# The end of the multi-head graph stage: TensorE's loop runs to the last chunk, its last heads stand between the last stage's first products, and sums and statistics move forward

## The reference

```python
x = _L0_gnn_ref(x, adj, ...)   # layer norm, 8-head attention, + Wo; layer norm, gelu(h Wf1) Wf2; residuals
# _L1_gnn_ref(x, bias=adj, ...)
attn_in = layer_norm(x, g1, b1)
attn = graph_attention(attn_in, bias, W1, a_src1, a_dst1) + x      # 8 heads of 32
attn_in2 = layer_norm(attn, g2, b2)
out = graph_attention(attn_in2, bias, W2, a_src2, a_dst2) + attn   # 1 head of 256
# graph_attention: h = x W; s = h.a_src; t = h.a_dst
#   softmax(leaky_relu(s_i + t_j, 0.2) + bias) @ h
```

## Time and profile before

| | |
|---|---|
| median of three runs | 1089.6 us |
| the profiled execution | 1089.35 us, of which the span of instructions 1087.5 us |
| PE busy | 1042.4 us, 96% of the span |
| DVE, ACT, POOL busy | 799.3, 713.7, 406.7 us |
| mean granted clock of PE | 0.990 |

### The profile page before, as it was taken

The page is one execution under the profiler, slowest core; times in us unless marked ns, Lnnn a source line. Parts: engine busy times, 40 slices in busy tenths (PEclk is TensorE's granted clock), DMA queues, the critical chain, the costliest instruction groups (busy, mean ns, idle before and its releaser), DMA issues.

```text
span 1087.5 us, 39257 instructions
## 1 busy us (share of the span) xinstructions
PE 1042.4 (96%) x15958; PEld 917.0 (84%) x15958; DVE 799.3 (74%) x1919; ACT 713.7 (66%) x1724; POOL 406.7 (37%) x642
## 2 busy tenths in 40 slices
PE   8999999999999998999999999999889999869997
PEld 7888888888888877899889988998778888768886
DVE  5677777777777787866665666545779988859996
ACT  4876777777677764544554455546678888847774
POOL 3711211211111113411131113212368888767773
PEclk9999999999999999999999999999999999989999
DMA  8211112211110002100110011010001000001222
GB/s 234 69 41 42 41 42 65 56 41 42 41 41 18 6 10 59 33 21 21 30 29 20 21 30 30 20 40 11 14 20 30 19 19 29 4 2 60 79 78 98
DMA packets 78520, 43.67 MB, mean 40 GB/s; under 512 B 38926, under 2 KB 74028, under 8 KB 78380
## 3 DMA queue, kind: packets, MB, share of 16 engines
q1 hardware_dynamic: 78360, 41.72, 14.1%
q10 hardware_dynamic: 20, 0.01, 0.0%
HBM read 21.25 MB, written 12.58 MB: 31 GB/s over the span
## 4 chain that ended last, share of the span: by engine, by line
PE 83%; issue 4%; DVE 4%; POOL 3%; SPq 3%; ACT 2%; DMA 1%; POOLq 0%; DVEq 0%; ACTq 0%
PE BK L1436 8%; PE BK L1438 8%; PE BK L1437 8%; PE BK L1588 6%; PE BK L1562 5%; PE BK L1717 5%; PE BK L1718 5%; PE BK L1719 5%; PE BK L1574 4%; PE BK L1555 3%; PE BK L1461 3%; PE BK L1452 3%; PE BK L1764 3%; PE BK L1886 2%; PE BK L1453 2%
## 5 line engine op out<-in xcount | busy, mean ns | idle before, releaser
L1270 ACT ACTIVATE gf<-BK,bcol 128x512 f32<-128x512 f32 x128 | 88.4, 691 | 156.4 <-PE BK L1438 143.2
L1041 POOL TENSOR_TENSOR ve<-mv,eps_l 128x4 f32<-128x4 f32 x64 | 18.1, 283 | 454.1 <-DVE mv L323 435.6
L1190 ACT ACTIVATE e_sb<-BK,nmx 128x128 f32<-128x128 f32 x512 | 142.4, 407 | 28.5 <-DVE nmx L535 28.5
L632 DVE TENSOR_TENSOR gl<-gf,gh 128x512 fp32r<-128x512 f32 x128 | 100.9, 790 | 64.3 <-ACT gh L1271 62.0
L1717 PE MATMUL BK<-wf_hi,gh 128*128 128x256 f32 x512 | 142.3, 278 | 0.3 <-DVE gl L632 0.2
L1718 PE MATMUL BK<-wf_hi,gl 128*128 128x256 f32 x512 | 141.7, 277 | 0.0
L1719 PE MATMUL BK<-wf_lo,gh 128*128 128x256 f32 x512 | 141.6, 277 | 0.0
L541 DVE TENSOR_TENSOR pt_sb<-BK,ft 128x512 f32<-128x512 f32 x128 | 85.2, 686 | 56.0 <-PE BK L1562 54.4
L1210 ACT ACTIVATE xn<-x_all,neg_mr,rstd 128x256 f32<-128x256 f32 (+1 forms) x188 | 103.4, 608 | 5.1 <-POOL neg_mr L1050 4.7
L1436 PE MATMUL BK<-xh,wf_hi 128*128 128x512 f32 x256 | 101.5, 396 | 2.8 <-DVE xl L352 2.8
L1438 PE MATMUL BK<-xh,wf_lo 128*128 128x512 f32 x256 | 101.5, 397 | 0.0
(11 more groups left out here) (214 smaller groups left out, 2768.0 us busy)
## 6 DMA issues: line engine op xcount, KB each, us to landing
out_dram<-y SPq DMA_DIRECT2D x16, 512.0 KB, 2.9
x_all<-in_x_dram SPq DMA_DIRECT2D x15, 512.0 KB, 4.6
xn<-tb_ln SPq DMA_DIRECT2D x240, 32.0 KB, 1.9
adj_in<-in_adj_dram SPq DMA_DIRECT2D x64, 64.0 KB, 3.5
adj_kept<-adj_tr SPq DMA_DIRECT2D x16, 256.0 KB, 2.5
adj_in<-adj_kept SPq DMA_DIRECT2D x16, 256.0 KB, 2.6
s_wf<-in_L_gnn_Wf_dram SPq DMA_DIRECT2D x2, 1024.0 KB, 7.4
x_all<-in_x_dram SPq DMA_DIRECT2D x2, 256.0 KB, 2.9
```

The source lines that it names most:

```text
L632: dve.tensor_tensor(gl[:, f, :], gf[f % 2][:], gh[:, f, :].bitcast(F32), ALU.subtract).then_inc(b_gl, 1)
L1190: e = act.activation(e_sb[:, j, :], LE[:, r, q, :], ACT.Exp, bias=nmx[:, j:j + 1], scale=1.0)
```

## The change

On PE the loop of the multi-head stage covers all chunks but the first two (`tail=0`); behind it the remaining heads of chunk 14 go around the ratios, the turn of chunk 1 for the last stage comes earlier, and the last four heads of chunk 15 stand in pairs between the high and the low products of the last stage's chunk 0. The wait for all of chunk 15's output copies (`c_ev`) moves from ahead of the last stage to its step 1.

On POOL the bias and the scale for chunk 2 (addition to chunk 0, L1018, and L1041 to L1050) move from behind both residuals to between those of chunk 14 and chunk 15. On DVE the aggregation and the next statistics move forward too, and a wait for POOL's last share of chunk 15 (`c_att`) comes in before step 1 writes y. DVE caps the row of chunk 1 instead of POOL. On ACT the normalisation of chunk 1 comes before the copies of chunk 14.

In the feed-forward stage, step 0 makes the low part of chunk 1, and normalises and turns chunk 2, after one addition instead of two; the marks come after the fourth addition, and the sums and scores in steps 1 and 2. The high parts of W1 and W2 (ACT) and their low parts (POOL) come one step later.

```diff
@@ DVE, feed-forward
-                    if g == 2 and not final:
+                    if g == (1 if i == 0 else 2) and not final:
                         turned_lo(i + CB + 1)
...
-                    if isinstance(i, int) and i == 0 and g < 2:
-                        (setup_marks, lambda: setup_sums(0, 0))[g]()
+                    if isinstance(i, int) and i == 0 and g == 3:
+                        setup_marks()
                     if isinstance(i, int) and i == 1 and g < 3:
-                        (lambda: setup_sums(0, 1), lambda: setup_scores(0), lambda: setup_sums(1, 0))[g]()
-                    if isinstance(i, int) and i == 2 and g < 2:
-                        (lambda: setup_sums(1, 1), lambda: setup_scores(1))[g]()
+                        (lambda: setup_sums(0, 0), lambda: setup_sums(0, 1), lambda: setup_scores(0))[g]()
+                    if isinstance(i, int) and i == 2 and g < 3:
+                        (lambda: setup_sums(1, 0), lambda: setup_sums(1, 1), lambda: setup_scores(1))[g]()
@@ DVE, end of the multi-head stage
             for h in range(4):
                 c_scale(NC - 1, h)
+            dve.wait_ge(ln_nm, nm_count(CD + 1, CD))
+            dve.wait_ge(ln_st, (CD + 3) * G)
+            aggr(CD + 2)
             c_recip(NC - 2, 1 - last)
...
             d_lo(1, 1, 1)
+            dve.wait_ge(ln_mv, (CD + 3) * G)
+            for g in range(G):
+                stats(CD + 3, 3, g)
             c_recip(NC - 1, last)
@@ DVE, last stage (the same work is taken out of step 0)
                 d_bias(i, par)
+                if at == 1:
+                    dve.wait_ge(c_att, NC * G + C_START)
...
-                if i == 0:
+                if i < 2:
                     d_cap(i)
@@ POOL
+                    if first == CD and i == 0:
+                        return
...
                     residual_sum(NC - 2)
+                    add_bias(0, CD, c2_bc, d_xb)
+                    pool.wait_ge(ln_xn, (CD + 2) * G)
+                    rstd_of(CD + 2, EPS[CD])
+                    neg_mean_of(CD + 2, CD)
                     residual_share(NC - 1, (NC - 1) % 2)
@@ ACT
+            normalise(0, CD, range(G))
             c_out_copy(NC - 2, 1 - last, 1)
             c_out_copy(NC - 2, 1 - last, 2)
-            normalise(0, CD, range(G))
-            c_out_copy(NC - 1, last, 0)
             d_hi(1, 1, 0)
             d_hi(1, 1, 1)
+            c_out_copy(NC - 1, last, 0)
@@ PE
-            looped(pe, c1_step)
+            looped(pe, c1_step, tail=0)
...
+            def first_product(g):
+
+                pe.wait_ge(c_pp, (NC - 1) * H + g + 6)
+                d_h_hi(0, 0, g)
+                d_h_hi(0, 0, g + 1)
```

More of the change, by code:

```diff
@@ L850, in c2_step @@
                 prev = (i - 1, half - (1 - par), 1 - par)
-                if ahead:
+                if ahead and i > 0:
                     dve.wait_ge(ln_nm, nm_count(i + CD + 1, CD))
@@ L855, in c2_step @@
                     d_norms(*older, 2, 3)
-                if ahead:
+                if ahead and i > 0:
                     aggr(i + CD + 2)
-                if far:
+                if far and i > 0:
                     dve.wait_ge(ln_mv, (i + CD + 3) * G)
@@ L1014, in add_bias @@
                 for g in range(G):
-                    if first == CD and g == 2 and i > 1:
+                    if first == CD and g == 2 and i > 2:
                         pool_cap(i - 1)
@@ L1094, in norms @@
                         setup_gain("w2", 28)
-                    if first == CB and isinstance(i, int) and i == 1:
+                    if first == CB and isinstance(i, int) and i == 2:
                         setup_lo("w1", False, 3)
@@ L1293, in b_step @@
                     turned_hi(i + CB + 1)
-                if isinstance(i, int) and i == 0:
+                if isinstance(i, int) and i == 1:
                     setup_hi("w1", False, 5)
@@ L1821, in _ @@
             pe.wait_ge(setup_pool, 7)
-            looped(pe, c1_step)
+            looped(pe, c1_step, tail=0)
             last = (NC - 1) % 2
+            c_av(NC - 2, 1 - last, 4)
+            c_av(NC - 2, 1 - last, 5)
             pe.wait_ge(ln_xl, (CD + 1) * KT)
             ratios(NC - 1, last, 0)
-            for h in range(4, H):
-                c_av(NC - 2, 1 - last, h)
-            ratios(NC - 1, last, 1)
-            for h in range(4):
-                c_av(NC - 1, last, h)
+            c_av(NC - 2, 1 - last, 6)
+            c_av(NC - 2, 1 - last, 7)
             pe.wait_ge(c_hb, NC * 2)
@@ L1833, in _ @@
             d_ln_turn(1, 1, 1)
-            for h in range(4, H):
-                c_av(NC - 1, last, h)
+            ratios(NC - 1, last, 1)
             def d_h_hi(i, par, g):
@@ L1890, in c2_step @@
                 more = back and not (isinstance(i, int) and i == NC - 1)
-                d_h_pair(i, par, 0)
+                if i == 1:
+                    pe.wait_ge(c_ev, NC * len(HEAD_GROUPS))
                 if back:
+                    d_h_pair(i, par, 0)
                     d_outer(i - 1, 1 - par)
-                d_h_pair(i, par, 2)
+                    d_h_pair(i, par, 2)
                 if back:
@@ L1903, in c2_step @@
                         d_av(i - 1, 1 - par, g)
-            pe.wait_ge(c_pp, NC * H)
-            pe.wait_ge(c_ev, NC * len(HEAD_GROUPS))
+            for h in range(4):
+                c_av(NC - 1, last, h)
+            first_product(0)
+            c_av(NC - 1, last, 4)
+            c_av(NC - 1, last, 5)
+            d_h_lo(0, 0, 0)
+            d_h_lo(0, 0, 1)
+            first_product(2)
+            c_av(NC - 1, last, 6)
+            c_av(NC - 1, last, 7)
+            d_h_lo(0, 0, 2)
+            d_h_lo(0, 0, 3)
             pe.wait_ge(d_clear, 3)
```

## The result

The changed kernel takes 1078.27 us (median of 4 runs, 1075.68 to 1080.96); the kernel before, on the same chip, 1089.19 (1086.77 to 1091.33). The ratio is 0.9895, with an interval of 0.9862 to 0.9929, so 0.7 to 1.4% faster. The forecast was 1076.5.

The account below looks back on a forecast made before the run. PE, the busiest engine, was taken to lose time to idling, page waits and half clock in feed-forward and at the seam into the last stage. 1089.35 minus 4.4 (feed-forward) minus 8.4 (seam) gave 1076.5 us, range 1072.5 to 1082.

Parts of the forecast that it names:

- Feed-forward, 4.4: Feed-forward stage: removed idle time and half clock save 4.4 us, bounds 2.6 to 4.5.
- idle 2.84 plus half clock 1.7: Before and in chunk 1's first products in feed-forward: PE's 2.84 us idle and the 1.7 us half-clock loss both go.
- bound of 0.2 for the addition behind the block turn: Feed-forward, DVE's addition for graph 1: PE's fourth product loses 0.2 us at most waiting for it.
- ACT's and POOL's setup moves into idle time: Feed-forward: the moved setup work of ACT and POOL was given no cost.
- The seam, PE: Between multi-head and last stage: heads end about 965.5, first d_av (end product of a chunk) at 972.0 instead of 979.90.
- the old 1.82 and 1.42: Old PE page stalls, taken as prices for two new ones, in heads 4 and 7 of chunk 15.
- The seam, POOL: Seam: POOL's offset of chunk 3 comes at 976.3 and ends ACT's wait; chunk 1's d_av comes 8.4 us earlier.
- starving seam: Rival, seam: two more page waits and a half-clock stretch leave 4.5 of the 8.4 us, 1080.4; chance 0.15.
- back edge: Rival, PE's multi-head loop: a taken branch costs a fetch, up to 1.82 us more, 1078.3; chance 0.02.
- half clock returned: Rival, feed-forward or last stage: half clock returns despite removed idle time, 1.7 us each, 1078.2 to 1079.9; chance 0.08.
- wait unseen before: Rival, seam: an unseen wait takes the seam's gain, leaving feed-forward's alone, 1085; chance 0.06.
- lasting half clock: Rival, seam into last stage: PE stays at the lower clock, 30 us costing 15.0, 1091.6; chance 0.04.

Follow-up runs that it names:

- e1: Only the feed-forward edits, on the kernel before; 1087.5 us, ratio 0.997 to before.
- e3: The changed kernel once more without an edit; 1076.95 us, ratio 0.9877 to before.
- e9: Changed kernel with POOL, in the last stage's step 1, making chunk 3's scale and offset ahead of its bias addition to chunk 1; 1079.32 us.
- e2: Only the seam's edits, feed-forward as in the kernel before; 1080.28 us, ratio 0.9913 to before.
- e7: Changed kernel with PE doing heads 4 to 7 of chunk 15 in one block before the last stage's first products; 1076.83 us, one run.
- e5: Changed kernel with POOL's share and sum of chunk 15 put back ahead of the addition to chunk 0 and chunk 2's scale and offset; 1082.96 us.
- e6: Changed kernel with PE's loop ending two chunks earlier again, chunks 14 and 15 written out; 1080.08 us, one run.
- e10: Changed kernel with DVE making feed-forward step 0's low part of chunk 1 after two additions again; 1077.45 us, ratio 0.991 to before.
- e12: The same kernel as e9 once more; 1075.79 us, ratio 0.9876 to before.
- e4: Changed kernel with both the e9 and e10 edits, and DVE's cap of chunk 1 behind its second y; 1076.33 us.
- e11: The same kernel as e4 once more; 1075.35 us, ratio 0.9867 to before.
- e8: Kernel before with 32 more idle matmuls at the very start of PE's list; 1086.34 us, one run.

## Why the prediction was right, and where it was not

**The time.** Forecast 1076.5, measured 1078.27 and 1076.95; the difference to the kernel before was forecast at 12.8 and measured at 10.9 and 13.0. The profiled execution of the result is at the upper end for a reason outside the change: its first 417.55 us, before anything changed, were 2.59 longer than in the profile of before. The intervals of the studies are 0.5 to 0.7% wide, so two kernels could not be told apart from 0.2% on, as I had put it.

**Feed-forward, 4.4: right in kind, too large.** The 2.84 of idle time and the half clock behind it went, and the stretch became 3.43 shorter; the other profiles with the new feed-forward give 3.17 (e1) to 4.19 (e3), apart from e9 with its slow products. The sum "idle 2.84 plus half clock 1.7" held up to chunk 2's first product: there the gain was 4.56 in e3, and 3.82 in the first profile, which had lost 0.77 on the way. Two terms failed. The bound of 0.2 for the addition behind the block turn was broken by 0.77, and by 0.52 in e1, since the low part hangs on a transfer that landed up to 1.2 us later than in the one trace I had. And "ACT's and POOL's setup moves into idle time" put at nothing a step that gives back 0.37 to 0.39 in the first profile, e1 and e3. I was also lucky to price the half clock with POOL's low parts moved away: without that move it was worth almost nothing, as e2 shows (333.13 with full clock and 0.84 less idle time).

**The seam, PE: order and places right, prices wrong.** The 1.82 went with the loop's longer reach. The page waits came 8 matmuls into head 4 of chunk 15 and five before the end of head 7, where the grid of 127 had given 9 and four. But I priced them at the old 1.82 and 1.42, and they took 0.22 and 0.75. I read a stall as what is left of a transfer after the work that stands in the page before it, and that work had changed: products with 258 columns stood between the short matmuls. No run measures the transfer itself, and between executions of the same order the two stalls vary too, 0.33 and 0.48 in e3. The block of heads in e7, which reaches the same page sooner, got 1.76. The heads ended only 1.1 us earlier than forecast, since the matmuls between the stalls took 1.1 longer than I had summed, and the first d_av came 18.91 us after chunk 15's step, not 20.3.

**The seam, POOL: right.** The offset of chunk 3 was to come at 976.3 on a clock in which chunk 15's step ended at 951.66, so 24.6 us behind it; it came 24.4 behind it, as the releaser of ACT's wait. For that reason the 2.3 us that the page waits had been priced too high did not reach the d_av of chunk 1. It stands 27.14 behind the step, where 28.04 was forecast; of the 0.9, 0.3 is the earlier offset, and 0.6 the way from there to PE, which took 2.8 where I had 3.4. e5 shows that none of the seam's gain stands without this chain, and e9 that it is still the next in line, worth 0.97. How much it gives alone no run shows.

PE was not quite full from there, as I had it: the step to the third d_av took 7.23 (985.77 minus 978.54) where it was 6.78 before, with 0.32 of it idle for y.

**The sum.** Up to the third d_av the seam gained 7.18, and 1.82 ahead of it: 9.0 against 8.4. Feed-forward gained 3.2 to 4.2 against 4.4. The errors nearly cancel.

**The rivals.** A starving seam did not occur: PE's longest wait before the first d_av is 0.83, and the clock stayed at 1.00. No cost of the back edge shows. The Trainium skill ("Runtime: NRT & Kernel Launch", section "Instruction fetch mechanics") has a taken branch out of the stored window force a fetch; here the loop ran one time more with no PE instruction packet up to 950 us and no stall behind the branch, so no run shows such a fetch. The half clock returned in the seam of some executions (e2, e5, e6, e10, e12) and not in others (the change twice, e4, e7, e9, e11): the same list of instructions can go either way, as e9 and e12 did, and it cost 0.66 us up to the third d_av in e10 and nothing in e12. In feed-forward no profile but that of before has it, not even e2 and e8 with 2.0 and 2.2 us of idle time. A wait unseen before, or a lasting half clock, did not come. Of the signs I named, "one stall of 1.4 to 1.9 near head 4 and one near head 7" was wrong in size only; the others held in the profiles.

## What to carry to other kernels

When two losses stand one behind the other (an idle time and a slow clock behind it), ask what the second hides before adding them: an engine that is slow at that place shows only when the clock is back. A stall at instruction pages can't be priced by what it cost in the old order: the same page gave 0.22 or 1.76 us. And the gain of reordering around a seam is set by the slowest chain through it: here 7.2 of 9.0 us went when POOL's four small instructions, with the bias ahead of them, stood in their old place, whatever the other engines did.

## What the runs showed of the hardware that I had not expected

- PE's stalls in straight-line code follow a grid of 127 matmuls with their weight loads, and move when 32 matmuls are put at the very start of the program, 900 us earlier. In the loop, from 840 us on, no such stall stands, and PE's instruction queue moves nothing.
- The half-clock stretches wander from execution to execution: besides the seam they lay mostly at 10 to 30 us, 768 to 812 and at the very end. The third stretch of the table took 201.9 to 206.5 us in the ten profiles with the longer loop, with nothing changed in it.
- DVE's low part of a gelu takes 0.7 us at most places. In the step in which POOL makes the low parts of W1 and W2, whichever that is, three in a row take 0.96 to 1.68 each, in all fourteen profiles.
- The time to feed-forward's first addition was 413.9 to 417.6 us over fourteen profiles, and one execution ran the 256-column products of feed-forward 4% slower at a granted clock of 1.00. Below 0.3% only many runs, or the same short stretch in several profiles, can tell two kernels apart: the 0.97 of POOL's edit is the same to 0.02 us in four profiles and hardly to be seen in the times.
